# A Mamba-2 layer and a ternary FFN on one core: loops written out, opening and passage reordered

## The chip, the core and the metric

The kernel runs on one core of a Trainium2 chip. The core has a TensorE (PE, matrix products), a VectorE (DVE), a ScalarE (ACT), a GpSimd (POOL) and a SyncE (SP), which here only issues DMAs. Each engine has its own instruction stream, in order; they meet at semaphores alone. The time is device microseconds (us) of one execution. All data start and end in HBM.

## The reference

Input u is 2 sequences of 2048 tokens with 512 features. The result is the second of two blocks, each a layer, a residual and a layer norm:

```python
x = layernorm(u + attn(u));  out = layernorm(x + ffn(x))
# attn: state space layer (Mamba-2, SSD), 8 heads of 128, state 64
z, xBC, dt = split(u @ W_in.T);  dt = softplus(dt + dt_bias)
x, B, C = split(silu(causal_conv4(xBC) + conv_b))
dA = dt * -exp(A_log)                       # per head
y = ssd(x * dt, dA, B, C) + x * D           # h[t] = exp(dA[t]) h[t-1] + B[t] (dt x)[t];  y[t] = C[t] h[t]
yg = y * silu(z)
attn = (yg * rsqrt(mean(yg*yg) + 1e-5) * norm_w) @ W_out.T
# ffn: three weights W (2048 x 512) made ternary
q(W) = clip(round(W / s), -1, 1) * s,  s = mean(|W|) + 1e-8
ffn = (silu(x @ q(W_up).T) * (x @ q(W_gate).T)) @ q(W_down).T
```

## The kernel before

**Blocks.** The 4096 tokens are 8 blocks of 512, alternating between the two sequences; `par` is the sequence. Attention runs as steps n = 0..7, one per block, FFN as steps t = -1..7; t = -1 with its eight units q = 0..7 and what stands just ahead of it is the passage from one to the other. Products of f32 data are made from f16 high and low parts, three matmuls for one: so every weight piece needs a high part (ACT, `w_hi`) and a low part (`w_lo`, `w_lo_head`, in before all on DVE). A head tile, x or z of one head, is 12 matmuls into one of three PSUM banks that are used in turn (`RING`); eight other products share the bank `p_turn` in the order of `USES`.

**A step** has four slots p = 0..3 of two heads each. In a slot PE makes x and z of heads 2p and 2p+1 and, for the two heads of the slot before, transposes x (`turn_x`), makes the chunk states (`states`) and the outputs (`outputs`). x of a head passes ACT `conv_in`, DVE `conv` (three taps), ACT `conv_tanh`, DVE `silu`; then ACT `x_dt` scales the transposed x by dt. Of the next block, slots 1 to 3 also make B, C (`cb_tile`, `cb_conv`, `cb_silu`, whose outputs are `b_ch` and `c_ch`; `turn_b` and `cb` on PE read them) and dt (`dt_first`, `dt_second`, `dt_third`, then the cumulated sums). `cum_turned` copies these sums to `cum_t`, SP stores them (`store_cum`) and loads them back broadcast over partitions (`load_cum`, four DMAs per slot); ACT needs them for the decays (`growth`, `decays`). In slot 1 of step n the out projection of block n-1 is made, four chunks (`chunk_out`), each followed on DVE by `residual` (which adds `u_tok`, loaded by SP `load_utok`), its statistics, and `normalise`; `store_x1` writes the result.

**Weights of the FFN.** Their mean magnitude needs all 24 pieces of 512 KB of `w_ffn`: `load_abs(i)` on SP brings piece i into one of two buffers, and ACT (even i) or DVE (odd i) sums it (`magnitude(i)`, tile `abs_sum`). `load_abs(i)` waits until magnitude i-2 is done:

```python
if i >= 2:
    sp.wait_ge(abs_ok[i % 2], i // 2)
```

SP issues its DMAs in order, so whatever stands behind such a wait stands still too. SP's order in steps 0 and 1: slot (0,3) ends with `load_abs(8)` to `(11)`; then, opening step 1, `store_cum(1)` and `load_cum(1,0)`, in slot (1,0) `load_abs(12)`, `load_abs(13)`, `load_cum(1,1)`, and then `load_u(2)` and two `load_utok`. `load_abs(18)` and `(19)` stand ahead of `store_x1(0,0)` and `load_utok(0,2)`. From step 2 on the weights are made ternary (`quantise`, `factor_sums`) and stored.

**The FFN** works on one unit q of a block in seven products of sums and differences of quarter matrices (as Strassen's: `product`, names c11, c12, c21, c22, s1, u2, u3 for what is combined; ACT `chain_read` copies a product out of PSUM, DVE `summed` combines). `x_high`, `x_low`, `turn_x` on SP (DMA transposes) and `x_sum` prepare a block's input. `last_chunk` and `attention_rest` carry the last block's attention through t = -1.

**Loops.** The order of the work is written out by hand, per engine. Steps 0, 1, 6 and 7 are straight code; steps 2 to 5 are a register loop of two steps on every engine, and so are FFN steps 2 to 5:

```python
step(0, 0); step(1, 1)
with eng.Fori(0, QN // 2) as i:
    step(i * 2 + Q0, 0)
    step(i * 2 + (Q0 + 1), 1)
step(NB - 2, 0); step(NB - 1, 1)
```

In them a wait compares with a register's value, and `wait_apart` adds an increment of a semaphore behind it.

## Time and profile before

| | us |
|---|---|
| median of 3 runs | 1370.12 (1369.99 to 1370.62) |
| profiled execution, its own time | 1370.94 |
| its span | 1369.2 |
| PE busy | 1333.5 (97% of the span) |
| DVE / ACT / POOL busy | 1041.0 / 784.3 / 650.3 |
| granted TensorE clock, mean | 0.996 |

The busy time of an engine is the sum of its instructions; what lies between them is idle time, and the trace names for each idle stretch the instruction whose semaphore ended it. Only idle time of the engine that bounds the kernel costs time by itself. A granted clock of 1.00 is 2.4 GHz, 0.50 is 1.2 GHz. The opening is the span's first 175 us (steps 0 and 1), the register loops follow, the passage lies at about 680 to 800 us, and the FFN fills the rest.

### The profile page before, as it was taken

To read this page: it belongs to the slowest core of one execution; us is meant where nothing else is said; L and a number is where in the kernel's file an instruction comes from. 1 tells how busy PE (TensorE), PEld (TensorE's weight loads), DVE (VectorE), ACT (ScalarE), POOL (GpSimd) and SP (SyncE) were. 2 spreads that over 40 slices of the span, in tenths; PEclk is the share of its full clock that TensorE was granted. 3 is DMA by queue.
4 is the path that set the end of the run, shared out by engine and by line. 5 is a ranking of instruction groups with operands and counts; after the bars stand their busy time and mean duration, and the time that the engine had idled before them with its cause. 6 is when DMAs were issued, how large, how long until landed. Compare 5 with 4: busy or idle time off the path is not lost.

```text
span 1369.2 us, 26933 instructions
## 1 busy us (share of the span) xinstructions
PE 1333.5 (97%) x9318; PEld 866.4 (63%) x9318; DVE 1041.0 (76%) x1857; ACT 784.3 (57%) x1561; POOL 650.3 (47%) x634
## 2 busy tenths in 40 slices
PE   7899999999999999999999999999999999999998
PEld 4455565655555646556556677777777767777774
DVE  7887887887878868788684877777777767777775
ACT  6796673874757828658474555454544545454441
POOL 0575364673755837536255534353443424353331
PEclk9899999999999999999999999999999999999999
DMA  8537334353442633424546332223122322222002
GB/s 245 167 132 228 131 110 116 89 160 101 126 127 82 174 88 99 150 86 147 142 115 214 88 118 56 72 63 85 48 62 67 74 68 56 73 62 55 32 25 69
DMA packets 162796, 143.83 MB, mean 105 GB/s; under 512 B 101344, under 2 KB 123232, under 8 KB 161504
## 3 DMA queue, kind: packets, MB, share of 16 engines
q1 hardware_dynamic: 162656, 142.05, 36.1%
q8 instruction: 78, 1.28, 0.4%
q14 instruction: 62, 0.51, 0.1%
HBM read 99.93 MB, written 27.39 MB: 93 GB/s over the span
## 4 chain that ended last, share of the span: by engine, by line
PE 80%; DVE 7%; issue 4%; DMA 3%; ACT 2%; POOL 2%; SPq 1%; POOLq 0%; DVEq 0%; ACTq 0%
PE ring L936 20%; PE ring L1151 15%; PE ring L965 8%; PE p_turn L1131 7%; PE p_y L1131 7%; PE p_st L1131 6%; PE p_seg L1131 5%; PE p_y L1009 3%; PE p_y L1017 2%; PE p_st L999 2%; DMA quant<-in_w_ffn 2%; PE p_turn L989 1%; DVE acc L1804 1%; PE ring L1188 1%; DVE abs_sum L1782 1%
## 5 line engine op out<-in xcount | busy, mean ns | idle before, releaser
L936 PE MATMUL ring<-u_split,weights 128*128 128x512 f16 x1620 | 375.0, 382 | 2.2 <-DVE x_ch L1809 2.0
L936 PEld LDWEIGHTS ring<-u_split,weights 128*128 128x128 f16 x1620 | 154.9, 99 | 171.9 <-issue 6.6
L1713 POOL TENSOR_TENSOR xdt<-xdt 128x512 f32<-128x512 f32 x64 | 100.6, 1571 | 340.0 <-DVE xdt L2175 340.0
L965 PE MATMUL ring<-w_out,raw 128*128 128x512 f16 x672 | 147.3, 379 | 0.2 <-issue 0.2
L1804 DVE SCALAR_TENSOR_TENSOR acc<-ring,taps,acc 128x511 f32<-128x511 f32 (+2 forms) x192 | 143.7, 749 | 4.5
L965 PEld LDWEIGHTS ring<-w_out,raw 128*128 128x128 f16 x672 | 65.7, 98 | 79.5 <-issue 0.7
L1359 ACT ACTIVATE xdt<-p_turn,dts 128x128 f32<-128x128 f32 x256 | 72.7, 375 | 70.3 <-PE p_turn L989 70.3
L1620 POOL TENSOR_TENSOR raw<-yg,raw 128x512 f16<-128x512 f32 x64 | 78.8, 1231 | 65.9 <-ACT raw L1389 65.8
L1615 POOL TENSOR_TENSOR yg<-y_ch,z_ch 128x512 f32<-128x512 f32 x64 | 81.4, 1273 | 41.4 <-DVE y_ch L1929 41.4
L1368 ACT ACTIVATE p_seg<-cum_rows,cum 128x128 f32<-128x128 f32 x256 | 80.8, 389 | 8.7 <-DVE seg L1907 8.7
L1591 POOL TENSOR_TENSOR rstd<-var_e,exponent 128x1 f32<-128x1 f32 x32 | 20.2, 631 | 118.4 <-DVE var_e L1952 118.4
L1312 ACT ACTIVATE ring<-acc 128x512 f32<-128x512 f32 x64 | 38.7, 604 | 64.7 <-DVE acc L1804 63.6
L1628 POOL TENSOR_TENSOR sq_sum<-sq_sum,sq 128x512 f32<-128x512 f32 x56 | 71.3, 1273 | 0.0
L1009 PEld LDWEIGHTS p_y<-seg,xdt 128*128 128x128 f32 x512 | 62.4, 192 | 6.7 <-DVE seg L1907 2.3
L1520 ACT ACTIVATE cum_g<-c_dec,tanh_scale 128x512 f32<-128x512 f32 x32 | 23.1, 722 | 73.4 <-DVE b_dec L2167 73.4
L1009 PE MATMUL p_y<-seg,xdt 128*128 128x128 f32 x512 | 63.4, 276 | 1.7 <-DVE seg L1907 1.6
L1520 ACT ACTIVATE cum_g<-b_dec,tanh_scale 128x512 f32<-128x512 f32 x32 | 23.1, 722 | 70.1 <-DVE c_dec L2167 69.6
L1907 DVE TENSOR_TENSOR seg<-p_seg,cb_mask 128x512 f32<-128x512 f32 x64 | 43.9, 685 | 19.4 <-ACT p_seg L1372 19.3
L1520 ACT ACTIVATE grow<-xdt,tanh_scale 128x512 f32<-128x512 f32 x64 | 45.9, 718 | 19.5 <-DVE xdt L2167 19.0
L1838 DVE SCALAR_TENSOR_TENSOR z_ch<-thz,ring 128x512 f32<-128x512 f32 x64 | 43.8, 684 | 16.6 <-ACT thz L1328 14.3
L1809 DVE SCALAR_TENSOR_TENSOR x_ch<-ring,acc 128x512 f32<-128x512 f32 x64 | 44.0, 688 | 14.4 <-ACT ring L1312 14.0
L2167 DVE TENSOR_TENSOR xdt<-grow,p_turn 128x512 f32<-128x512 f32 x64 | 44.0, 687 | 13.3 <-ACT grow L1511 8.3
(395 smaller groups left out, 3246.7 us busy)
## 6 DMA issues: line engine op xcount, KB each, us to landing
cum_rows<-cum_dram SPq DMA_DIRECT2D x64, 256.0 KB, 4.1
quant<-in_w_ffn SPq DMA_DIRECT2D x24, 512.0 KB, 4.4
quant<-in_w_ffn SPq DMA_DIRECT2D x48, 256.0 KB, 4.1
cum_g<-cum_dram SPq DMA_DIRECT2D x64, 128.0 KB, 4.4
rows<-in_u_tok SPq DMA_DIRECT2D x32, 256.0 KB, 4.5
x_dram<-rows SPq DMA_DIRECT2D x32, 256.0 KB, 2.1
tern_ug<-quant SPq DMA_DIRECT2D x32, 256.0 KB, 3.3
u_raw<-in_u_t SPq DMA_DIRECT2D x7, 1024.0 KB, 8.7
```

The lines of the kernel that those rows point to most:

```text
L936: mm = pe.matmul(bank_k[:, :], w_in[:, ws, k, col:col + P], us[:, par, k * T:(k + 1) * T], start=(i == 0), stop=(i == 3 * KD - 1))
L965: mm = pe.matmul(ring[b][:, :], ys[:, h, c * P:(c + 1) * P], w_out[:, ws, h, :], start=(h == 0 and ys is y_hi and ws == 0), stop=(h == H - ...
L1009: pe.matmul(p_y[q][:, c * P:(c + 1) * P], xdt[:, q, c, :], seg[:, q, c, :], start=(c == 0), stop=False, skip_group_check=True)
L1131: mm = pe.matmul(bank_j[:, w * 256:(w + 1) * 256], factor(weight, w, k, q), xs[par][i][:, k, :], start=(first and w == 0 and k == 0 and xs ...
L1151: mm = pe.matmul(p_down[c % 2][:, :], hidden_tile(par, m, low)[:, c * P:(c + 1) * P], t_down(m), start=(e == 0 and m == 0 and not low), st ...
L1359: ins = act.activation(xdt[:, q, c, :], p_turn[:, c * P:(c + 1) * P], ACT.Copy, scale=dts[:, owner, c, h:h + 1])
L1368: ins = act.activation(p_seg[:, c * P:(c + 1) * P], cum_b[:, (2 * p - 2 + q) % 4, c, :], ACT.Relu, bias=cum[:, owner, h, c:c + 1], scale=-1.0)
L1520: act.activation(th[second], up, ACT.Tanh, scale=tanh_scale[:, 0:1]).then_inc(tanh_ok, 1)
L1615: pool.tensor_tensor(yg[:, q, :], y_ch[:, q, :], z_ch[:, k % 4, :], ALU.mult).then_inc(yg_ok, 1)
L1620: pool.tensor_tensor(y_lo[:, h, :], yg[:, q, :], y_hi[:, h, :], ALU.subtract).then_inc(ylo_ok, 1)
L1713: pool.tensor_tensor(tile_[:, 1, :, :], tile_[:, 0, :, :], tile_[:, 1, :, :], ALU.mult).then_inc(hid_ok, 1)
L1804: dve.scalar_tensor_tensor(acc[:, buf, k + 1:T], own[:, 0:T - 1 - k], taps[:, h, 2 - k:3 - k], acc[:, buf, k + 1:T], ALU.mult, ALU.add).th ...
```

## The change

**No loops.** `run_steps` and `ffn_steps` call `step` for each n and t in turn, on all five engines; every wait is on a constant, `wait_apart` and its increments are gone.

```diff
-            step(0, 0)
-            step(1, 1)
-            with eng.Fori(0, QN // 2) as i:
-                step(i * 2 + Q0, 0)
-                step(i * 2 + (Q0 + 1), 1)
-            step(NB - 2, 0)
-            step(NB - 1, 1)
+            for n in range(NB):
+                step(n, n % 2)
```

**Opening.** The low parts of heads 2, 3 and 7 are made by POOL in two instructions each, 2 and 3 first in its stream, 7 between the scaling and the low part of the first half of `w_out`. `cb_silu` makes b_ch first, and PE's `turn_b` waits for that alone, `cb` for all three. DVE's slot (0,2) is written out. The pieces below are of GpSimd, PE and DVE, in this order:

```diff
+            def w_lo_head(h):
+                own, k = raw_head(h), POOL_HEADS.index(h)
+                pool.wait_ge(w_hi_ok, head_piece(h) + 1)
+                pool.tensor_scalar(own, own, SW, None, ALU.mult).then_inc(w_mul_ok, 1)
+                pool.wait_ge(w_mul_ok, k + 1)
+                pool.tensor_tensor(w_in[:, 1, :, 2 * P * h:2 * P * (h + 1)], own, w_in[:, 0, :, 2 * P * h:2 * P * (h + 1)],
+                                   ALU.subtract).then_inc(w_half_ok, 1)
...
             def turn_b(n, use):
-                wait_apart(pe, bc_ok, n * 3 + 3, passed["pe"])
-                wait_apart(pe, turn_free, use, passed["pe"])
+                wait(pe, bc_ok, n * 3 + 1)
+                wait(pe, turn_free, use)
...
             cum_turned(0, turn_use(0, "cumt0"))
-            w_lo_head(2, w_half_ok)
-            cb_silu(0, 0, p_y[0])
+            cb_silu(0, 0, p_y[0], False)
             z_gate(0, 0)
-            w_lo_head(3, w_lo_ok)
+            conv(0, 0, 1)
             b_read(0, 0, turn_use(0, "b0"))
-            conv(0, 0, 1)
+            c_silu(0, 0, p_y[0])
...
+            magnitude(1)
             w_lo(4)
-            magnitude(1)
-            w_lo(5)
-            cb_conv(1, 1, ring[ring_bank("cb", 0)])
-            dt_second(1)
+            def second_slot():
+                n, par, p = 0, 0, 2
+                skip(n, p, 0)
+                skip(n, p, 1)
+                state_update(n, par, p - 1, C - 1)
+                cb_conv(1, 1, ring[ring_bank("cb", 0)])
+                dt_sum(1)
+                within(n, par, p, 0)
+                cb_silu(1, 1, ring[ring_bank("cb", 0)])
...
+                conv(n, par, 2 * p)
+                b_read(1, 1, turn_use(0, "b"))
+                dt_third(1, 1)
+                silu(n, 2 * p)
+                z_gate(n, 2 * p)
+                cum_read(1, 1, turn_use(0, "cum"))
+                w_lo_head(6)
+                conv(n, par, 2 * p + 1)
```

The slot of DVE at n = 0, p = 2 before, from its first `y_ch` (the skip term of the outputs) on; `carry` is the last chunk's state, `acc` the convolution:

```order
L1929 SCALAR_TENSOR_TENSOR y_ch<-x_ch,d_skip,p_y 128x512 [waits y_full]
L1929 SCALAR_TENSOR_TENSOR y_ch<-x_ch,d_skip,p_y 128x512
L1921 SCALAR_TENSOR_TENSOR carry<-st,grow,p_st 128x128 [waits st_ok]
L1907 TENSOR_TENSOR seg<-p_seg,cb_mask 128x512 [waits e_ok]
L1829 SCALAR_TENSOR_TENSOR c_ch<-ring,acc 64x512 [waits thc_ok]
L1829 SCALAR_TENSOR_TENSOR c_ch<-ring,acc 64x512
L1831 SCALAR_TENSOR_TENSOR b_ch<-ring,acc 64x512
L1782 TENSOR_REDUCE abs_sum<-quant 128x1 [waits abs_in1]
L1799 SCALAR_TENSOR_TENSOR acc<-ring,taps,corr 128x3 [waits acc_ok]
L1801 COPY halo<-ring 128x3
L1804 SCALAR_TENSOR_TENSOR acc<-ring,taps,acc 128x511 [waits tap_ok]
L1804 SCALAR_TENSOR_TENSOR acc<-ring,taps,acc 128x510 [waits tap_ok]
```

And after; the convolution with L1848 is that of B and C, which stood ahead of the slot before:

```order
L1966 SCALAR_TENSOR_TENSOR y_ch<-x_ch,d_skip,p_y 128x512 [waits y_full]
L1966 SCALAR_TENSOR_TENSOR y_ch<-x_ch,d_skip,p_y 128x512
L1958 SCALAR_TENSOR_TENSOR carry<-st,grow,p_st 128x128 [waits st_ok]
L1843 SCALAR_TENSOR_TENSOR acc<-ring,taps,corr 128x3 [waits accc_ok]
L1845 COPY halo<-ring 128x3
L1848 SCALAR_TENSOR_TENSOR acc<-ring,taps,acc 128x511 [waits tapc_ok]
L1848 SCALAR_TENSOR_TENSOR acc<-ring,taps,acc 128x510 [waits tapc_ok]
L1848 SCALAR_TENSOR_TENSOR acc<-ring,taps,acc 128x509 [waits tapc_ok]
L1893 TENSOR_SCALAR dt_w<-dt_e 128x32 [waits dt_a]
L1944 TENSOR_TENSOR seg<-p_seg,cb_mask 128x512 [waits e_ok]
L1855 SCALAR_TENSOR_TENSOR b_ch<-ring,acc 64x512 [waits thc_ok]
L1863 SCALAR_TENSOR_TENSOR c_ch<-ring,acc 64x512 x2
```

The skips and the carry have moved ahead of the convolution of B and C, and b_ch ahead of c_ch; the magnitude behind b_ch is gone from here.

The odd magnitudes stand one place later (`odd_rows`). Before, those of slot (0,2) were 3 and 5, of (0,3) 7 and 9, of (1,0) 11 and 13, of (1,1) 15, 17 and 19; now they are 3, then 5 and 7, then 9 and 11, then 13, 15, 17 and 19. Ahead of the second `cum_t` of DVE's stream, that of block 1, four rows of `abs_sum` stood, now three. In slot (1,1) magnitude 17 has a place of its own behind the dt steps. DVE there before, from `dt_w` on (`rows` with `mv,rstd` is `normalise`, with `ring,rms` is `residual`; `utok_in0` is the load of u_tok):

```order
L1859 TENSOR_SCALAR dt_w<-dt_e 128x32 [waits dt_a]
L1861 TENSOR_SCALAR dt_m<-dt_w 128x32 [waits dt_v]
L1863 RECIPROCAL dt_r<-dt_m 128x32 [waits dt_v]
L1956 TENSOR_SCALAR rows<-rows,mv,rstd 128x512 [waits rstd_ok]
L1944 SCALAR_TENSOR_TENSOR rows<-ring,rms,rows 128x512 [waits x1_out0,utok_in0,chunk_full]
L1947 BN_STATS stats<-rows 128x6 [waits chunk_ok]
L1949 BN_AGGR mv<-stats 128x2 [waits stat_ok]
L1952 TENSOR_SCALAR var_e<-mv 128x1 [waits mv_ok]
L1782 TENSOR_REDUCE abs_sum<-quant 128x1 [waits abs_in1]
```

And after:

```order
L1893 TENSOR_SCALAR dt_w<-dt_e 128x32 [waits dt_a]
L1898 TENSOR_SCALAR dt_m<-dt_w 128x32 [waits dt_v]
L1900 RECIPROCAL dt_r<-dt_m 128x32 [waits dt_v]
L1809 TENSOR_REDUCE abs_sum<-quant 128x1 [waits abs_in1]
L1993 TENSOR_SCALAR rows<-rows,mv,rstd 128x512 [waits rstd_ok]
L1981 SCALAR_TENSOR_TENSOR rows<-ring,rms,rows 128x512 [waits x1_out0,utok_in0,chunk_full]
L1984 BN_STATS stats<-rows 128x6 [waits chunk_ok]
L1986 BN_AGGR mv<-stats 128x2 [waits stat_ok]
L1989 TENSOR_SCALAR var_e<-mv 128x1 [waits mv_ok]
L1809 TENSOR_REDUCE abs_sum<-quant 128x1 [waits abs_in1]
```

A magnitude now stands ahead of `normalise(0,1)` and `residual(0,2)`, beside the one behind the statistics.

On SP in the same steps `load_wout(1)` has moved ahead of `load_abs(4)`, and `load_cum(1,1)` ahead of `load_abs(13)`; `store_cum(1)` stays behind `load_abs(11)`, and `store_x1(0,0)` with `load_utok(0,2)` behind `load_abs(19)`. In ACT's slot (0,2) `cb_tanh(1)` and `x_dt` of the second head stand ahead of `conv_in(4)`, `dt_ln(1)` ahead of the magnitude, and `conv_in(5)` ahead of the gating.

**Passage.** On SP (step 7, slot 2) the store and load of a chunk of block 6 stand between the transposes of block 0's input:

```diff
                             if is_at(n, NB - 1):
-                                for j in range(4):
+                                for j in range(2):
                                     turn_x(0, 0, j)
                             store_x1(n - 1, 0)
                             load_utok(n - 1, 2)
                             if is_at(n, NB - 1):
-                                turn_x(0, 0, 4)
+                                for j in range(2, 4):
+                                    turn_x(0, 0, j)
                             store_x1(n - 1, 1)
                             load_utok(n - 1, 3)
+                            if is_at(n, NB - 1):
+                                turn_x(0, 0, 4)
```

PE makes product 5 ahead of product 6, ACT reads u3 and s1 ahead of gating heads, and at t = -1 `residual` 0 and 3 stand ahead of the sum c12 on DVE, residual 3 at q = 7 instead of 6. POOL makes rms ahead of `hidden` there. The pieces are of PE, ACT, the table of `attention_rest`, POOL and DVE:

```diff
             product(0, 0, 0, 1, True)
+            pe.wait_ge(turn_free, turn_use(NB, "x01") + 1)
+            product(0, 0, 0, 5, True)
             pe.wait_ge(s1_ok, 1)
             product(0, 0, 0, 6, False)
-            pe.wait_ge(turn_free, turn_use(NB, "x01") + 1)
-            product(0, 0, 0, 5, True)
...
             gated(NB, 0, 1)
+            chain_read(0, 0, u3, prod[7], u3_ok, c21_ok)
             act.wait_ge(scales_ok, 3)
             gated(NB, 1, 0)
+            chain_read(0, 1, s1, prod[1], s1_ok, c11_ok)
             gated(NB, 1, 1)
...
-            return {2: 0, 3: 1, 4: 2, 6: 3}.get(q) if is_at(t, -1) else None
+            return {2: 0, 3: 1, 4: 2, 7: 3}.get(q) if is_at(t, -1) else None
...
                         if is_at(t, -1) and q == 2:
                             pool.wait_ge(ms_ok, 1)
                             pool.tensor_tensor(rms[:, :], ms[:, :], exponent[:, :], ALU.pow).then_inc(rms_ok, 1)
...
+                        hidden(m, k, True)
                         hidden(m, k, False)
...
+                    if attention_rest(t, q) in (0, 3):
+                        residual(NB - 1, attention_rest(t, q), p_down[attention_rest(t, q) % 2])
                     if before:
                         summed(m, k, "c12", u2, u2_ok, 5, ALU.add)
```

At t = -1 also the first half of `hidden` stands ahead of `x_low` on DVE, and `x_high` behind the first `hidden_tanh` on ACT. In step 7, slot 1, DVE makes `normalise` 0 and `residual` 1 ahead of `x_low` 2 and 3.

## Rows read from the trace of the kernel before

**Rows 1.** The page's summary: busy us, share of the span and instructions of each engine.
```profile
PE 1333.5 (97%) x9318; PEld 866.4 (63%) x9318; DVE 1041.0 (76%) x1857; ACT 784.3 (57%) x1561; POOL 650.3 (47%) x634
```

**Rows 2.** Waits of PE, costliest first: line, releaser, us in total, times, longest.
```profile
PE p_turn L974 <- DVE b_ch L1831: 4.6, 2, 4.0
PE p_st L999 <- DVE carry L1921: 4.3, 2, 2.3
```

**Rows 3.** PE in order of time, opening: start, us, line, operation, idle and releaser.
```profile
63.87 0.69 PE L974 MATMUL p_turn<-ident,b_ch 64*128 64x64 f32 x4 [3.97 <-DVE b_ch L1831]
...
73.36 0.81 PE L936 MATMUL ring<-u_split,weights 128*128 128x512 f16 x3
...
112.66 0.63 PE L989 MATMUL p_turn<-ident,x_ch 128*128 128x128 f32 x4 [0.18 <-ACT xdt L1359]
```

**Rows 4.** PE in order of time, its gaps in the rest of the run.
```profile
362.72 0.65 PE L989 MATMUL p_turn<-ident,x_ch 128*128 128x128 f32 x4 [0.98 <-issue]
...
689.29 0.99 PE L999 MATMUL p_st<-xdt,b_dec 128*64 128x128 f32 x14 [2.33 <-DVE carry L1921]
...
724.29 0.94 PE L1131 MATMUL ring<-b_tok,weights 128*128 128x256 f16 x7 [0.69 <-ACT cum_g L1511]
...
735.03 1.05 PE L1131 MATMUL p_turn<-c_ch,weights 128*128 128x256 f16 x8 [1.37 <-DVE xdt L2167]
...
754.33 2.76 PE L1188 MATMUL ring<-w_out,raw 128*128 128x512 f16 x12 [1.54 <-DVE rows L1944]
...
792.79 1.05 PE L1131 MATMUL p_turn<-c_ch,cum_rows 128*128 128x256 f16 x8 [1.45 <-DVE xdt L2167]
...
1105.36 0.83 PE L1131 MATMUL p_st<-acc,weights 128*128 128x256 f16 x6 [1.63 <-issue]
```

**Rows 5.** Two stretches: us, busy time of each engine, granted clock, DMA share, GB/s.
```profile
33.00:36.00 3.00, 3.00 (x9) 1.04 (x8) 2.93 (x7) 2.99 (x2) 0.00 (x0) 0.50 1.03 322
...
60.00:67.00 7.00, 3.13 (x10) 1.39 (x11) 5.11 (x9) 3.18 (x7) 2.71 (x4) 0.51 0.71 193
```

**Rows 6.** DVE in order of time, opening, step 1 and the passage.
```profile
25.70 0.69 DVE L1831 SCALAR_TENSOR_TENSOR b_ch<-p_y,acc 64x512 f32<-64x512 f32 x1
...
47.43 2.29 DVE L1770 SCALAR_TENSOR_TENSOR weights<-raw,weights 128x2048 f16<-128x2048 f32 x1
...
50.77 3.24 DVE L1770 SCALAR_TENSOR_TENSOR weights<-raw,weights 128x2048 f16<-128x2048 f32 x1
...
105.09 1.21 DVE L1782 TENSOR_REDUCE abs_sum<-quant 128x1 f32<-128x1024 f32 x1
...
146.09 0.75 DVE L1944 SCALAR_TENSOR_TENSOR rows<-ring,rms,rows 128x512 f32<-128x512 f32 x1
...
154.28 1.40 DVE L1929 SCALAR_TENSOR_TENSOR y_ch<-x_ch,d_skip,p_y 128x512 f32<-128x512 f32 x2
...
680.35 0.75 DVE L1944 SCALAR_TENSOR_TENSOR rows<-ring,rms,rows 128x512 f32<-128x512 f32 x1 [3.03 <-DMA rows<-in_u_tok]
```

**Rows 7.** POOL in order of time: low parts of the first half of w_out.
```profile
48.38 7.76 POOL L1672 TENSOR_TENSOR w_out<-rows,w_out 128x512 f16<-128x512 f32 x4 [3.79 <-ACT w_out L1289]
```

**Rows 8.** DMA issues of the queue engine SP in order of time, steps 0 and 1.
```profile
95.39 0.43 SPq L606 DMA_DIRECT2D cum_dram<-cum_t  x1
99.47 0.34 SPq L616 DMA_DIRECT2D cum_rows<-cum_dram  x1
...
104.85 0.33 SPq L598 DMA_DIRECT2D quant<-in_w_ffn  x1
...
140.05 0.43 SPq L622 DMA_DIRECT2D rows<-in_u_tok  x1
```

**Rows 9.** ACT in order of time, step 1 and the passage.
```profile
110.87 0.62 ACT L1351 ACTIVATE grow<-cum_g 128x512 f32<-128x512 f32 x1
...
733.61 0.58 ACT L1511 ACTIVATE grow<-ring 128x512 f32<-128x512 f32 x1
```

**Rows 10.** The page's DMA issues: tiles, engine, count, KB each, us to landing.
```profile
rows<-in_u_tok SPq DMA_DIRECT2D x32, 256.0 KB, 4.5
```

More of the change, by code:

```diff
@@ L1458, in step @@
                         decays(n, par, p, 0)
-                    if not end:
+                    if is_at(n, 0) and p == 2:
+                        cb_tanh(1, ring[ring_bank("cb", 0)])
+                        x_dt(n, par, p, 1)
                         conv_in(n, 2 * p)
-                    if state_slot(n, p):
+                        decays(n, par, p, 1)
+                        dt_ln(1)
+                    elif not end:
+                        conv_in(n, 2 * p)
+                    if state_slot(n, p) and not (is_at(n, 0) and p == 2):
                         x_dt(n, par, p, 1)
                         decays(n, par, p, 1)
-                    if is_at(n, 0) and p == 2:
-                        cb_tanh(1, ring[ring_bank("cb", 0)])
                     if abs_rows(n, p, 0) is not None:
@@ L1474, in step @@
                         split_u(n + 1, 1 - par)
-                    if p == 2 and more(n):
+                    if p == 2 and more(n) and not is_at(n, 0):
                         dt_ln(n + 1)
@@ L1478, in step @@
                         magnitude(abs_rows(n, p, 1))
-                    if not end:
+                    if not end and not (is_at(n, 0) and p == 2):
                         conv_in(n, 2 * p + 1)
@@ L1551, in ffn_step @@
                         m, its, k = before
+                    if before and not (is_at(t, -1) and q == 1):
                         wait(act, act_ok, 2 * (m * NQ + k) - 1)
@@ L1700, in step @@
                         rms_root(n - 1, turn_use(n, "ssq"))
-                    if quantised(n) and not isinstance(n, int):
+                    if quantised(n) and n < NB - 2:
                         factor_sums(n, p)
@@ L1827, in cb_silu, with c_silu @@
                     dve.wait_ge(cdec_ok, n * NP - NP)
+                dve.scalar_tensor_tensor(b_ch[:, :], b[N:P, :], 1.0, acc[N:P, 2, :], ALU.add,
+                                         ALU.mult).then_inc(bc_ok, 1)
+                if both:
+                    c_silu(n, par, b)
+            def c_silu(n, par, b):
                 for half in range(2):
@@ L2046, in _ @@
             dt_first(1, turn_use(0, "dt"))
+            magnitude(1)
             w_lo(4)
[L2048 to L2051 removed]
+            def second_slot():
[7 more added lines that the diff above has]
+                cb_silu(1, 1, ring[ring_bank("cb", 0)])
+                dt_inverse(1)
+                for c in range(C - 1):
+                    state_update(n, par, p, c)
+                within(n, par, p, 1)
+                conv(n, par, 2 * p)
[6 more added lines that the diff above has]
+                conv(n, par, 2 * p + 1)
+                silu(n, 2 * p + 1)
+                magnitude(3)
+            second_slot()
             def step(n, par):
                 first, end = is_at(n, 0), is_at(n, NB)
[L2055 removed]
+                for p in range(3 if first else 0, 4):
                     if gate_slot(n, p):
@@ L2065, in step @@
                         within(n, par, p, 0)
-                    if first and p == 2:
-                        cb_silu(1, 1, ring[ring_bank("cb", 0)])
-                    if abs_rows(n, p, 0) is not None:
-                        magnitude(abs_rows(n, p, 0) + 1)
                     if not end:
@@ L2143, in step @@
                         dt_second(n + 1)
+                    if odd_rows(n, p, 2) is not None:
+                        magnitude(odd_rows(n, p, 2))
                     if p == 1 and not first:
@@ L2258, in ffn_step @@
                         summed(n, q, "c11", s1, s1_ok, 2, ALU.add)
+                    if is_at(t, -1) and before:
+                        hidden(m, k, True)
                     for j in splits_at(t, q):
@@ L2268, in ffn_step @@
                     if before:
-                        hidden(m, k, True)
+                        if not is_at(t, -1):
+                            hidden(m, k, True)
                         hidden(m, k, False)
```

195 lines of the change are left out of this document (103 added, 92 removed).

## The prediction

> **What bounds the kernel now.** I read the engine summary first. TensorE (PE) is busy 97% of the span [rows 1], so only time in which PE stands still, or runs slower, can be won. The waits by engine come next: PE waits 4.6 us for b_ch and 4.3 us for a carry [rows 2], always two waits together. Then PE in order of time, which puts them: 3.97 us of the b_ch wait lies at 63.87, so z of head 5 starts only at 73.36 [rows 3]; 2.33 us of the carry wait stands ahead of 689.29 [rows 4]. Outside the first 175 us, the passage from attention to FFN (680 to 800 us) and the last 9 us PE has no gap over 0.3 us but two: 0.98 us at 362.72 and 1.63 us at 1105.36, put down to "issue" [rows 4]; there the register loops of PE and the other engines turn. Last the granted clock by stretch: it is 0.50, 1.2 GHz, at 33 to 36 us and 0.51 on average at 60 to 67 us, each after or around a PE idle [rows 5].
>
> **Part 1: no loops.** PE's two boundary gaps go: -0.98 and -1.63 us. The extra semaphore increments and register arithmetic sit on queues that PE does not wait for (the steps inside the loops show no "issue" gap over 0.3 us), so I take nothing for them. The whole part is -2.6 us. The lower bound is those gaps, since what the other engines lose there is behind PE's work; the upper one is zero, if the gap is PE fetching a far stretch of code that straight code fetches too. I take -2.6, because steps 0, 1, 6 and 7, already straight code, have no such gap in PE's rows. The Trainium skill says the same from the other side (Runtime: NRT & Kernel Launch, Instruction fetch mechanics): a taken branch breaks the sequential prefetch, so straight code has no such stall; by it the term is the whole -2.6 as well.
>
> **Part 2: the opening.** b_ch comes first on DVE, the low parts of heads 2, 3 and 7 leave DVE, and its slot (0,2) is written out. Walked forward with the durations of before:
> - b_ch stood behind a low part (1.2) and two c_ch (1.4) and started at 25.70 [rows 6]; PE's turn_b moves up by 0.7. With two low parts of a head less on DVE (1.2 each), z of head 2 moves up by 2.8 and x of head 4, which needs w_lo(4), by 3.4, to 47.7.
> - w_lo(5), 3.24 us at 50.77, is gone and the skips stand ahead of the B/C convolution, so states(0,2) moves up by 5.5 to 53.3, and turn_b(1) from 63.87 to 54.4; head 5's z starts at 61.3 instead of 73.36, 12.1 us earlier. Here DVE and ACT are late in turn: conv 5 has been put behind dt_third, cum_read and the low part of head 6, so the next turn_x moves up by 8.8 only, to 69.5. PE stands about 2.5 us before it and some of the next tiles run at half clock. The gain that arrives at step 1 is 8.3 to 9 us.
>
> One row bears on this sum: w_lo(5) took 3.24 us where w_lo(4), the same shape, took 2.29, and it ran while POOL did the four low parts of w_out in 7.76 us [rows 6, 7]. The Trainium skill (SBUF — State Buffer, SBUF: two separate sides) says that a DVE instruction with two SBUF inputs and a GpSimd one reading SBUF exclude each other for a whole instruction. By it, and the trace agrees with its 3.24 against 2.29, head 7's POOL part beside w_lo(4) would take up to 0.95 us of the gain at x of head 4; what I take is none, and the next part shows why it would not reach the end.
>
> **Queue block A.** The odd magnitudes come one place later on DVE: ahead of the second cum_t there are now three, not four. SP issues DMAs in order, and a load_abs(i) waits for magnitude i-2. load_abs(11), ahead of store_cum(1), now waits for magnitude 9, which sits where magnitude 11 stood, 105.09 [rows 6], less the 8.3 gained: it ends at 98.0. store_cum goes at 98.5 instead of 95.39; it lands 4.1 later by before (95.39 to the first cum_rows at 99.47 [rows 8]), 2.2 in the first block, so I take 3.1: four loads end at 103.6. Only then load_abs(12), at 104.85 before [rows 8]; it lands 4.4 to 5.2 later, 108.0 to 108.8. ACT does magnitude 12 ahead of growth(1,1) and x_dt, 110.87 before [rows 9]. So growth starts at 109.6 to 110.4, and PE's turn_x, 112.66 before [rows 3], at 111.4 to 112.1: of 8.3 us some 0.5 to 1.3 are left. PE idles about 8 us here, and the two stretches of 1.2 GHz (3.0 and 3.5 us long, costing half of that each [rows 5]) say that the clock falls after such a gap: +1.4. Balance after A: -0.5 + 1.4, about +1.
>
> **Queue block B.** magnitude 17 now stands after the dt steps of step 1, ahead of normalise(0,1) and residual(0,2), at 145.6 to 146.8. load_abs(19) waits for it, and behind it on SP stand store_x1(0,0) and load_utok(0,2), issued at 140.05 before [rows 8], now at 147.65. With 3.9 to 4.5 us to land (4.5 is the page's median [rows 10]) it is there at 151.5 to 152.2, and residual(0,2), 146.09 before [rows 6], waits for it. Behind it on DVE: its statistics (1.0), magnitude 19 (1.2), normalise (0.55), residual 3 with statistics (1.8), 0.66 for rstd and normalise 3. skip(1,2) comes at 158.5, not 154.28 [rows 6]: +4.2. PE's states had 1.3 us in hand, cum_proj behind it less: +2.9 there, +3.7 to 4.1 in all. B costs +4 (2.5 to 5). From step 2 on DVE catches up and PE keeps the loss.
>
> Opening together: +5; from -1, where either block is half as bad, to +8 with another stretch at 1.2 GHz.
>
> **Part 3: the passage.** PE's gaps, and what is late next:
> - 2.33 at 689.29 [rows 4]: the carry stood behind residual 2, which waited 3.03 us for its u_tok at 680.35 [rows 6], a load behind four transposes on SP. Now only two lie ahead. All 2.33 go.
> - 0.69 at 724.29: product 5 now fills it. 1.37 at 735.03: xdt waited for ACT's u3 at 733.61, behind the gating of two heads [rows 4, 9]; moved ahead of them it is done by 730. 1.54 at 754.33: the last chunk waited for a residual that waited for POOL's rms, which now goes ahead of a hidden of 1.65 us. 1.45 at 792.79: DVE's xdt stood behind residual 3.
> - Two small ones between the first and the second, 0.6 together, move with the first.
>
> Sum -8.0. But at q=7 of t=-1 residual 3 is now ahead of c12 and takes 0.75 plus 1.0 us of statistics there: +1.1. Residual 0 ahead of c12 at q=2 does the same unless rms is early. I take -6 (-3 to -7.5).
>
> **Sum.** The profiled execution took 1370.94 us. -2.6 + 5 - 6 = -3.6 gives 1367.3; it lay 0.8 over the median of the runs shown (1370.12), so by the median 1366.5. I say 1366.4.
>
> **Rivals.**
> - The queue blocks don't bite, because the DMAs land sooner than I took or magnitudes 9 and 17 are early enough: then 8 us stay from the opening, and with -2.6 and -6 it is 1353 to 1358. For it: the walk to 63.87 rests on durations alone. Against it: the SP queue is in order, and both waits are plain in the order. 0.13.
> - Nothing that can be measured: the passage only gives 3 of its 8, since PE waits for c12 or for the down product's residual instead, and the opening costs 4: 1367.5 to 1372.5. For it: each passage gap is under 2.4 us and the next producer is often 0.5 to 1 us behind. 0.28.
> - Slower: SP's in-order queue. If store_cum takes its 4.1 us (+1), B costs 5 (+1), and PE runs two further stretches of 3.0 to 3.5 us at 1.2 GHz behind these idles (+1.7 each), the opening is +10.4. Against -2.6 and the least that I allow the passage, -3, that is +4.8: 1375 (1373 to 1376). It decides from an opening of +8.3 on. For it: both waits are plain in the order, and neither is hidden behind another engine's work. Against it: PE's idle and the low clock overlap in part. 0.12.
> - The change doesn't do what it says in part 1: straight code stalls as the loop did; then 1369, within the second rival.
>
> **From these to the numbers.** Forecast (1360 to 1367.4) 0.47. A run can tell from no change about 0.2%, 2.7 us. Faster: 0.47 + 0.13 = 0.60; same 0.28; slower 0.12. Range 1357 to 1373: below it most of the first rival, above it most of the last. The forecast's own range is 1362 to 1369.
>
> **What would show it.** Loops: no "issue" gap of PE near 362 or 1105. Opening: turn_b(1) at about 54, head 5's z at about 61, a PE gap of some 8 us ending near 112 with a DMA of w_ffn ahead of it; store_cum(1) issued at 98, not at 87; load_utok(0,2) near 147.6 and DVE's residual waiting for it. If PE has no gap near 104 to 112, the first rival holds. Passage: states at the place of 689.29 without a gap, xdt no longer behind u3, a small new PE gap at q=7. It is wrong if block 1's loads land before ACT needs them, or if the passage keeps gaps of more than 4 us in sum.

## The result and the profile after

The changed kernel takes 1372.93 us, the median of 11 executions (1370.55 to 1373.87), against 1370.12 (1369.70 to 1371.08): the ratio is 1.0017, with a 95% interval of 1.0009 to 1.0025. It is slower by 2.8 us, where 3.7 us less were forecast; a second set of 11 executions gave 1373.35 against 1370.32 (ratio 1.0018, 1.0009 to 1.0027). Its profiled execution took 1370.55 us with a span of 1368.4, less than all others of both sets: the trace shows the change at its best, and what the others have beside it is a question of its own, below.

Where PE stands at the same piece of work in the two traces:

| work | before | changed | difference |
|---|---|---|---|
| z of head 5 | 73.36 | 62.35 | -11.0 |
| turn_x(1,1,1) | 112.66 | 113.51 | +0.9 |
| states(1,2) | 157.22 | 162.49 | +5.3 |
| product of the magnitudes' sums | 171.38 | 177.75 | +6.4 |
| first tile behind the loop's boundary | 363.21 | 368.54 | +5.3 |
| states(7,2) | 689.29 | 692.37 | +3.1 |
| chunk 1 in the passage | 754.33 | 752.48 | -1.9 |
| product at q = 7 of t = -1 | 792.79 | 791.60 | -1.2 |
| first product behind the FFN loop's boundary | 1105.36 | 1104.21 | -1.2 |

The opening won 11 us by 73 us and was 0.9 behind at 113. PE in order of time in the changed kernel, at the places of [rows 3] and behind them (in brackets the idle time ahead and what ended it):

```profile
55.36 0.46 PE L973 MATMUL p_turn<-ident,b_ch 64*128 64x64 f32 x4
...
62.35 2.76 PE L935 MATMUL ring<-u_split,weights 128*128 128x512 f16 x12
...
113.51 1.08 PE L989 MATMUL p_turn<-ident,x_ch 128*128 128x128 f32 x4 [8.72 <-ACT xdt L1359]
114.38 3.84 PE L935 MATMUL ring<-u_split,weights 128*128 128x512 f16 x12
...
162.49 1.09 PE L999 MATMUL p_st<-xdt,b_dec 128*64 128x128 f32 x16 [3.52 <-DVE carry L1958]
```

turn_b(1) has no wait left. But a gap of 8.72 us has come ahead of turn_x(1,1,1), the 12 matmuls behind it take 3.84 us where they take 2.75 elsewhere, and states(1,2) waits 3.52 us for a carry. What each waits for shows first on SP, answering to [rows 8] (the second number is the issue's own time):

```profile
99.02 0.98 SPq L601 DMA_DIRECT2D cum_dram<-cum_t  x1
102.75 0.33 SPq L611 DMA_DIRECT2D cum_rows<-cum_dram  x1
...
105.49 0.58 SPq L593 DMA_DIRECT2D quant<-in_w_ffn  x1
...
149.70 0.42 SPq L617 DMA_DIRECT2D rows<-in_u_tok  x1
```

and on ACT, answering to [rows 9]:

```profile
110.18 1.06 ACT L1293 ACTIVATE quant<-quant 128x1024 f32<-128x1024 f32 x1 [8.45 <-DMA quant<-in_w_ffn]
...
111.71 0.62 ACT L1351 ACTIVATE grow<-cum_g 128x512 f32<-128x512 f32 x1
```

and on DVE, answering to [rows 6]; the first row is magnitude 9:

```profile
97.40 1.21 DVE L1809 TENSOR_REDUCE abs_sum<-quant 128x1 f32<-128x1024 f32 x1
...
154.31 0.75 DVE L1981 SCALAR_TENSOR_TENSOR rows<-ring,rms,rows 128x512 f32<-128x512 f32 x1 [5.34 <-DMA rows<-in_u_tok]
...
160.69 1.40 DVE L1966 SCALAR_TENSOR_TENSOR y_ch<-x_ch,d_skip,p_y 128x512 f32<-128x512 f32 x2
```

store_cum(1) goes at 99.02, behind load_abs(11), which magnitude 9 releases at 98.5; its loads go from 102.75, and load_abs(12) at 105.49. ACT is through with its work at 101.7 and stands 8.45 us for that piece, with growth(1,1) and x_dt behind it, and PE behind x_dt. In the second block load_utok(0,2) goes at 149.70 instead of 140.05 and residual(0,2) waits 5.34 us for it.

The passage's gaps, answering to [rows 4]:

```profile
692.37 1.09 PE L999 MATMUL p_st<-xdt,b_dec 128*64 128x128 f32 x16
...
752.48 2.75 PE L1188 MATMUL ring<-w_out,raw 128*128 128x512 f16 x12
...
791.60 1.05 PE L1131 MATMUL p_turn<-c_ch,cum_rows 128*128 128x256 f16 x8 [1.50 <-DVE xdt L2222]
...
795.30 1.05 PE L1131 MATMUL p_turn<-u_raw,u_split 128*128 128x256 f16 x8 [0.90 <-DVE c_dec L2222]
...
797.20 1.05 PE L1131 MATMUL p_seg<-u_raw,u_split 128*128 128x256 f16 x8 [0.85 <-ACT cum_g L1518]
```

Those at 689.29, 724.29, 735.03 and 754.33 are gone, that at 792.79 has stayed with 1.50 us, and two new ones of 0.90 and 0.85 us stand behind it. A third new one, 0.53 us on DVE's xdt, stands at 765.57.

### The profile page after: what moved, and what is told of

Same layout as the page of the kernel before. It is cut to its first block, busy times and chain, and to the rows that moved or that the text cites. A ratio compares the mean times of both kernels' runs of the same rounds, so it can differ in the third digit from the quotient of the medians.

```text
span 1368.4 us, 24907 instructions
## 1 busy us (share of the span) xinstructions
PE 1331.5 (97%) x9318; PEld 867.0 (63%) x9318; DVE 1046.1 (76%) x1855; ACT 785.2 (57%) x1561; POOL 666.7 (49%) x640
## 4 chain that ended last, share of the span: by engine, by line
PE 82%; DVE 8%; issue 4%; ACT 2%; POOL 2%; DMA 1%; SPq 0%; POOLq 0%; DVEq 0%; ACTq 0%
PE ring L935 20%; PE ring L1151 15%; PE ring L964 9%; PE p_turn L1131 7%; PE p_y L1131 7%; PE p_st L1131 6%; PE p_seg L1131 6%; PE p_y L1009 3%; PE p_y L1017 2%; PE p_st L999 2%; PE p_turn L989 2%; DVE acc L1831 1%; PE ring L1188 1%; DMA raw<-in_w_in 1%; POOL sq_sum L1643 1%
## 5 line engine op out<-in xcount | busy, mean ns | idle before, releaser
L1307 ACT ACTIVATE acc<-ring,tap_bias,taps 128x512 f32<-128x512 f32 x64 | 49.5, 774 | 6.7 <-PE ring L935 6.4
```

## The experiments

Each kernel was timed beside the kernel before on the same chip; the median of the latter was 1370.32 for e1 to e4, 1370.31 for e5 to e8, 1369.86 for e9 to e12 and 1370.39 for e13 and e14. So a difference of two medians from different groups carries up to some 0.5 us of its surroundings; where that matters, the difference from the kernel before is given instead. "A" is the block at 113 us, "B" that at 162.

### The change once more

No edit; a second trace.

> The changed kernel once more, unaltered, for a second trace: its profiled execution took 1370.55 us, but the median of its eleven runs is 1372.93 and the mean granted clock of the others is 0.990 to 0.995 against 0.997. Theory (clock after an idle): PE's idle of 8.7 us ahead of 113.5 us and that of 3.5 us ahead of 162.5 come in every execution, and how long PE then runs at 1.2 GHz differs between executions; so a trace of a run near 1373 has the same gaps on all engines and one or two more stretches of 3 to 7 us at a granted clock of 0.50, worth 2 to 3 us, behind these gaps. Rival (DMA): the slower executions have longer landings of w_ffn and u_tok, so the gaps themselves are 1 to 2 us longer at the same clock. Rival (code): the slower executions have 'issue' gaps of PE in the steps that were loops. Time 1372 to 1373.5.

1373.35 us (1371.12 to 1374.55, 11 runs). The profiled execution is a long one, span 1371.9. PE in it, and then the granted clock of both traces by stretch (us, busy times of the five engines, granted clock, DMA share, GB/s):

```profile
115.22 1.08 PE L989 MATMUL p_turn<-ident,x_ch 128*128 128x128 f32 x4 [9.66 <-ACT xdt L1359]
...
165.31 1.97 PE L999 MATMUL p_st<-xdt,b_dec 128*64 128x128 f32 x16 [3.97 <-DVE carry L1958]
```

```profile
60.00:80.00 20.00, 16.94 (x103) 9.21 (x102) 17.40 (x36) 16.88 (x39) 14.59 (x14) 0.91 0.45 148
...
106.00:121.00 15.00, 5.78 (x24) 2.89 (x26) 4.45 (x9) 8.69 (x24) 4.65 (x5) 0.66 0.94 296
...
160.00:175.00 15.00, 11.03 (x73) 7.00 (x70) 13.93 (x32) 9.36 (x19) 7.80 (x9) 0.77 0.57 179
```

```profile
60.00:80.00 20.00, 16.80 (x116) 10.14 (x116) 17.41 (x35) 17.50 (x41) 14.71 (x14) 1.00 0.41 140
...
106.00:121.00 15.00, 7.49 (x41) 3.96 (x42) 5.77 (x11) 10.76 (x28) 4.47 (x5) 0.77 0.87 286
...
160.00:175.00 15.00, 11.44 (x88) 7.80 (x89) 14.03 (x31) 11.37 (x21) 8.62 (x9) 1.00 0.67 211
```

The same gaps, 0.4 to 0.9 us longer; but the clock is 0.91, 0.66 and 0.77 (the first three rows) where the short execution has 1.00, 0.77 and 1.00. states(1,2), 1.09 us there, takes 1.97 here. Both theories have a share: the gaps differ a little, and this execution ran at 1.2 GHz behind the gaps at 71 and 162 us too. Of the 22 executions of the change two have a mean clock of 0.997, and they are the two fastest, 1370.55 and 1371.12; the rest lie at 0.990 to 0.995. No new gap put down to "issue" is there: the third theory falls.

### The loops, and the passage, by themselves

e2 writes out the two loops and changes nothing else; with the loops go the register comparisons and the extra increments in their waits. e3 adds all the edits of the passage to that. Of e2's edit, the attention loop:

```diff
-            with eng.Fori(0, QN // 2) as i:
-                step(i * 2 + Q0, 0)
-                step(i * 2 + (Q0 + 1), 1)
...
+            for n in range(NB):
+                step(n, n % 2)
```

> The kernel before with the register loops written out on all five engines and nothing else. Theory: the two boundary gaps of PE (0.98 and 1.63 us) go: 1367.0 to 1367.8, that is -2.3 to -3.0. Rival (straight code costs its own fetches): within 0.5 us of 1370.1, with new issue gaps of PE somewhere in steps 2 to 5. Rival (the loops hid a phase that now meets a slower clock): slower than 1371.

> As e2 with the reordered passage as well, the opening left as it was before. Theory from the two profiles: the passage alone gives 4.7 us on PE (PE was 5.3 us late ahead of it and 0.6 behind it), so 1362 to 1363.5; the opening of the change is then shown to cost 9 to 11 us by the medians. Rival (the passage gives what it gives only because the opening came late to it): 1365 to 1367.

e2: 1367.88 (1366.96 to 1368.68), ratio 0.9980 (0.9971 to 0.9989), -2.4 us, 0.1 above the range of its theory. The boundary in its trace, at the place of 362.72:

```profile
361.52 0.60 PE L978 MATMUL p_turn<-ident,x_ch 128*128 128x128 f32 x4
```

No gap, as forecast; the one at 1105.36 is gone too. e3: 1362.95 (1362.60 to 1363.50), ratio 0.9942 (0.9928 to 0.9955). The passage gives 4.9 us more, and the opening of the change, 1373.35 against 1362.95, costs 10.4. (The three terms add up to the whole change by the way they are taken, one after the other, so their sum checks nothing.)

### The two moves on the queue

e4 makes both, e5 that for A, e6 that for B. The diff shows the lines at their new places; the same lines are taken out at the old ones.

```diff
                         load_abs(10)
+                        store_cum(n + 1, 1 - par, turn_use(n, "cumt"))
+                        load_cum(n + 1, 1 - par, 0)
                         load_abs(11)
...
                         load_abs(18)
+                        store_x1(0, 0)
+                        load_utok(0, 2)
                         load_abs(19)
```

> The changed kernel with two moves on the queue engine alone: store_cum(1) and load_cum(1,0) ahead of load_abs(11), and store_x1(0,0) with load_utok(0,2) ahead of load_abs(19). Theory (the two queue blocks): PE's gap of 8.7 us at 113.5 shrinks to 1 to 3 us, since ACT's magnitude 12 gets its piece at about 104 instead of 110; residual 2 no longer waits 5.3 us at 154.3. PE at step 2 is then 6 to 8 us earlier than in the change before, and no stretch of 1.2 GHz stands behind 113: 1360 to 1364. Rival (the gap is DMA bandwidth, not the queue's order): the landing of w_ffn pieces and of the cum rows gets longer by as much, and it stays within 2 us of 1372.9.

> The changed kernel with the first of the two moves alone: store_cum(1) and load_cum(1,0) ahead of load_abs(11). Theory: PE's gap at 113.5 falls from 8.7 to about 3 us and the stretch at 1.2 GHz behind it gets shorter; residual(0,2) still waits some 5 us for its u_tok, since PE comes to block 2 earlier and DVE's magnitude 17 moves with it: 1366.5 to 1368.5. Rival (the second block takes back what the first gives, because load_abs(19) waits for a fixed DMA chain): within 1.5 us of 1373.

> The changed kernel with the second move alone: store_x1(0,0) and load_utok(0,2) ahead of load_abs(19). Theory: the gap at 113.5 stays at 8.7 to 9.7 us, residual(0,2) no longer waits 5.3 us, states(1,2) comes without its 3.5 to 4.0 us gap, and the stretch at 1.2 GHz that one of two traces shows behind that gap is gone: 1368.5 to 1370.5. Rival (B costs nothing by itself, DVE is as late without it): within 1 us of 1373.

e4 1364.12 (1362.82 to 1365.12), e5 1366.77 (1364.74 to 1368.38), e6 1368.92 (1367.24 to 1371.78). Against 1373.35 that is -9.2, -6.6 and -4.4. e5 and e6 lie inside what the theory gave, e4 0.1 above its upper edge; the rivals, all within 1 to 2 us of 1373, fall. With the magnitudes where the change has them, the order of the queue decides whether there is a block. The two moves do not add: 6.6 and 4.4 by themselves, 9.2 together, so the move for B is worth 4.4 with block A in place and 2.6 without it (why was not tested). In e5 and e6 the other block is still there, as the rows of PE show, of e5 first:

```profile
108.94 1.09 PE L991 MATMUL p_turn<-ident,x_ch 128*128 128x128 f32 x4 [3.97 <-ACT xdt L1361]
...
158.75 1.97 PE L1001 MATMUL p_st<-xdt,b_dec 128*64 128x128 f32 x16 [3.22 <-DVE carry L1960]
```

```profile
114.40 1.08 PE L992 MATMUL p_turn<-ident,x_ch 128*128 128x128 f32 x4 [9.32 <-ACT xdt L1362]
```

In e5 A has shrunk to 3.97 and B, 3.22, is nearly whole; in e6 A is whole and states(1,2) has no wait. What is left of A in e5 is ACT's magnitude 12, which stands 3.70 us for its piece of w_ffn in the trace. e8 moves that magnitude too:

```diff
-                     (1, 0): (None, 10, 12), (1, 1): (None, 14, 16, 18)
+                     (1, 0): (None, 10), (1, 1): (12, 14, 16, 18)
```

> As e4 with one more edit: ACT's magnitude 12 moves from the end of slot (1,0) to behind the decays of slot (1,1), so that growth(1,1) and x_dt do not stand behind its piece of w_ffn (in e4's trace it waited 2.9 us for it, and PE 3.15 us for x_dt, with 3 us at 1.2 GHz behind). Theory: that gap goes, 1360 to 1362 against e4's 1364.1. Rival (the pieces of w_ffn are a chain of their own: each later magnitude is a later load, and a DVE or ACT wait comes back further on): 1363 to 1365.

Four executions took 1358.13 to 1360.47, median 1359.8, 0.2 below the theory's range; a fifth took 4920, which nothing in its record explains, and is left out of the median. The gap ahead of turn_x(1,1,1) is gone in its trace.

### The magnitudes' places

e7 takes the change and puts the odd magnitudes where they were, the queue's order as in the change; e10 takes e3, opening and queue as before, and puts them one place later. Of e7:

```diff
-            rows_ = {(0, 3): (5, 7), (1, 0): (9, 11), (1, 1): (13, 15, 17, 19), (1, 2): (21, 23)}
+            rows_ = {(0, 3): (7, 9), (1, 0): (11, 13), (1, 1): (15, 17, None, 19), (1, 2): (21, 23)}
...
+                magnitude(3)
                 conv(n, par, 2 * p)
...
-                magnitude(3)
+                magnitude(5)
```

> The changed kernel with the odd magnitudes on DVE where they stood before (3 and 5 in slot (0,2), 7 and 9 in (0,3), 11 and 13 in (1,0), 15, 17 and 19 in (1,1)), the order of the queue engine as in the change. Theory (the later magnitudes are what blocks the queue): load_abs(11) is released by magnitude 9 near 86, store_cum goes at 87 to 88, both blocks are gone without touching the queue's order: 1361 to 1365; magnitude 3 ahead of conv(4) costs 1.2 us of DVE in a slot where PE waits for ACT anyway. Rival (the pieces land too late for such early magnitudes, so DVE waits for DMA in slot (0,2)): 1366 to 1370.

> e3 (no loops, reordered passage, opening as before) with one edit: the odd magnitudes on DVE one place later, exactly as in the change. Theory (this move alone makes both queue blocks): magnitude 9 ends near 106, store_cum goes behind it at 107 instead of 95.4, the loads of the cumulated sums come near 111 and ACT's growth(1,1) and PE's turn_x(1,1,1) at about 120 instead of 112.7; residual(0,2) waits for its u_tok too: 1372 to 1378, that is 9 to 15 over e3's 1363. Rival (the blocks need the earlier opening of the change to show): 1363 to 1366.

e7: 1360.42 (1360.30 to 1361.72), a little below what was expected; 12.9 us come back by this one edit; store_cum goes at 88.72 in its trace. e10: 1386.48 (1385.47 to 1386.84, four executions), +23.5 on e3, beyond the 9 to 15 expected. Its rows, of SP, then of POOL, then of PE:

```profile
75.31 0.43 SPq L586 DMA_DIRECT2D rows<-in_w_out  x1
...
112.14 1.12 SPq L601 DMA_DIRECT2D cum_dram<-cum_t  x1
```

```profile
81.45 4.03 POOL L1671 TENSOR_TENSOR rows<-rows,norm_s 128x512 f32<-128x512 f32 x4 [8.76 <-DMA rows<-in_w_out]
```

```profile
89.78 2.07 PE L1007 MATMUL p_y<-seg,xdt 128*128 128x128 f32 x8 [4.38 <-DVE seg L1915]
...
128.37 1.08 PE L987 MATMUL p_turn<-ident,x_ch 128*128 128x128 f32 x4 [10.22 <-ACT xdt L1357]
...
177.96 1.98 PE L997 MATMUL p_st<-xdt,b_dec 128*64 128x128 f32 x16 [3.48 <-DVE carry L1929]
```

The direction holds and the two blocks are the ones named, but magnitude 9 ends at 111.7, not at 106, since a third block stands ahead of them, 4.38 us at 89.78, with low clock behind it. Its rows show the queue once more: e10 has the queue of before, where load_wout(1) stands behind load_abs(5) and so behind magnitude 3, which is now later. It goes at 75.31, in e3 at 64.58; POOL waits 8.76 us for it with the scaling of w_out, ACT and DVE stand behind POOL's yg (3.73 and 4.97 us), and PE behind DVE. The change has moved this load ahead of load_abs(4), where it goes at 57.98. No run moves it by itself, so this third block is read from the rows and has no price of its own. The edit on the magnitudes costs 12.9 with the opening and queue of the change and 23.5 with those of before. So the reordered opening without this edit is worth 1362.95 - 1360.42 = 2.5 us, not the 8 to 9 that stand at 100 us: z of head 5 stands at 63.39 in e7, 9.1 us earlier than in e3, and the product of the magnitudes' sums at 167.60, 3.2 us earlier (170.76).

### The clock behind the gap

e9 is the change with 36 matmuls more in gap A, e13 is e6 with the same.

```diff
+                    if is_at(n, 1) and p == 1:
+                        pe.wait_ge(y_ok, n * H)
+                        for i in range(36):
+                            pe.matmul(p_y[0][:, :], w_in[:, 0, 0, 0:P], u_hi[:, par, 0:T], start=True, stop=True)
```

> The changed kernel with 36 further matmuls on PE (128x512, f16, about 7.8 us) in the gap ahead of turn_x(1,1,1), into the bank that the outputs of that slot overwrite later; their results are not used. They start once the skips of the slot are done (105.0 in the change's trace) and would end at about 113. Theory (the clock falls after the idle, and how long it stays low differs between executions): the granted clock stays 1.00 over 106 to 121, PE's next 12 matmuls take 2.75 us and not 3.84, and the median falls by 1.5 to 3 to 1370 to 1371.5. Rival (the low clock is not tied to this idle): the clock is 0.5 in the same stretch and the time is 1373 or more.

> e6 (only store_x1(0,0) and load_utok(0,2) moved ahead of load_abs(19)) with the 36 further matmuls of e9 in PE's remaining gap ahead of turn_x(1,1,1). e6 measured 1368.92 (1367.24 to 1371.78). Theory (the gap costs its own 8.7 us and then 1 to 2.5 us of low clock, different in each execution): with the gap filled the granted clock is 1.00 from 106 us to 175 us and the median is 1366.5 to 1367.5. Rival (the clock falls anywhere, this gap or not): 1368.5 to 1369.5.

e9: 1371.37 (1370.01 to 1375.54), 2.0 below the change by the medians as they stand, 1.5 when each is taken from the kernel before beside it. e13: 1367.66 (1367.01 to 1369.06), 1.3 below e6 by either way and 0.2 above the theory's 1367.5, and within 2.1 us where e6 spread over 4.5 (2.8 without its slowest one). PE in e9, then the clock in e9 and in e6:

```profile
106.59 7.94 PE L1090 MATMUL p_y<-u_split,weights 128*128 128x512 f16 x36 [0.91 <-DVE y_ch L1970]
115.26 0.63 PE L989 MATMUL p_turn<-ident,x_ch 128*128 128x128 f32 x4 [0.73 <-ACT xdt L1363]
115.72 2.75 PE L935 MATMUL ring<-u_split,weights 128*128 128x512 f16 x12
```

```profile
106.00:121.00 15.00, 13.49 (x74) 6.49 (x75) 4.82 (x10) 9.00 (x25) 4.87 (x5) 1.00 0.96 305
...
160.00:175.00 15.00, 12.24 (x85) 8.30 (x86) 13.53 (x30) 11.12 (x21) 8.88 (x9) 0.89 0.65 211
```

```profile
106.00:121.00 15.00, 6.60 (x33) 3.37 (x34) 4.46 (x9) 9.43 (x26) 4.17 (x5) 0.66 0.94 298
```

More work on PE in a gap makes the kernel faster, since the tile behind it takes 2.75 us and not 3.84 to 4.57. e9 still has B, and the clock there is 0.89; e13 has neither, and its clock is 1.00 from 106 to 175 us (its mean clock is 0.998 to 0.999 in all 11 executions, e6's 0.993 to 0.996).

### What is left, and the best version

e11 is e3 with residual 3 back at q = 6. e12 is the change with magnitudes 3 to 9 as before, 11 alone in (1,0), 13 to 19 in (1,1), and the move for B. e14 is e12 with the edits of e8 and e11.

```diff
-            return {2: 0, 3: 1, 4: 2, 7: 3}.get(q) if is_at(t, -1) else None
+            return {2: 0, 3: 1, 4: 2, 6: 3}.get(q) if is_at(t, -1) else None
...
+            rows_ = {(0, 3): (7, 9), (1, 0): (11,), (1, 1): (13, 15, 17, 19), (1, 2): (21, 23)}
```

> e3 with residual 3, its norm_root and normalise at q = 6 behind the sums, as before, the rest of the passage as in the change. It asks where the passage's missing 1.3 to 1.8 us went. Theory: the two new gaps of PE at q = 7 (0.90 on c_dec and 0.85 on ACT's p_seg read) are from residual 3 ahead of c12 and go: 1361 to 1361.8. Rival (they come from the end of the passage, the gap of 1.45 comes back beside them): 1363 to 1364.

> The change with magnitudes 3 and 5 in slot (0,2), 7 and 9 in (0,3) as before, but only 11 in (1,0) and 13, 15, 17, 19 in (1,1), and with store_x1(0,0) and load_utok(0,2) ahead of load_abs(19). In e7's trace DVE waited 4.7 us for piece 13 at the end of slot (1,0), with PE 1.9 and 0.9 us behind; here that wait goes. Theory: 1357 to 1359. Rival (the pieces are a chain, the wait comes back at magnitude 17 or 19): 1360 to 1362.

> e12 with ACT's magnitude 12 behind the decays of slot (1,1) (as in e8) and residual 3 at q = 6 (as in e11): all that the runs so far pointed to. Theory: e12 has no PE gap over 0.4 us between 76 and 160 us, so magnitude 12 gives nothing more, and residual 3 gives 0.3 to 1.2: 1359 to 1360. Rival (magnitude 12 behind the decays makes ACT late in slot (1,1)): 1360 to 1362.

e11: 1362.60 (1361.41 to 1362.96), above the theory's 1361.8 and 0.35 below e3, inside the spread of both (against the kernel before beside it, 7.3 below where e3 is 7.4 below). In its trace the two new gaps are gone, and the one on xdt has grown:

```profile
785.37 1.05 PE L1123 MATMUL p_turn<-c_ch,cum_rows 128*128 128x256 f16 x8 [2.06 <-DVE xdt L2167]
```

Against e3's 1.50, 0.90 and 0.85 us that is 1.2 us less in the trace; the medians don't confirm so much. e12: 1360.06 (1358.80 to 1361.09), above the 1357 to 1359 of the theory and no better than e7. The number is the rival's, but its wait is not there: PE has no gap over 0.4 us between 76 and 160 us. e12 reaches the tiles at 85 us some 1.8 us later than e7, and its trace has a stretch of low clock at 20 to 23 us that e7's has not; which of its edits makes it late was not tested. e14: 1358.76 (1357.31 to 1358.91), ratio 0.9910 (0.9896 to 0.9923): faster than both kernels, 11.6 us below the one before and 14.6 below the change, and 0.2 below what was expected. It is 1.7 below e7, which needs the one edit alone; four kernels (e7, e8, e12, e14) lie within that.

## Why the prediction was wrong

**The total.** 1366.4 was forecast, 1372.93 measured. By medians the three terms are -2.4 (forecast -2.6), -4.9 (forecast -6) and +10.4 (forecast +5). Loops: right. Passage: right in sign and place, 1.1 too much. The step that failed is the sum of the opening: "+5" from block A with its clock term (about +1) and block B (+4). Its mechanisms came; its sizes were too small. The traced executions show +6.4 at the product of the magnitudes' sums: PE reaches turn_x(1,1,1) 0.9 us late where -0.5 was forecast, the low clock behind costs 1.5 where 1.4 was forecast, and B brings the rest. Most of what is missing from there to +10.4 lies between the traced executions and the medians: the change's trace is 2.4 us faster than its median, that of before 0.8 us slower. So the term that was most mis-sized is, as far as the second trace of the change shows it, the low clock behind the idles, put at one stretch (+1.4) from one trace, with the arrival of block A (1.4) next. How much of those 3 us is low clock alone stays open in part: filling one gap gives 1.3 to 2.0 of them back.

**The walk to 73 us** held to 1.2 us: turn_b(1) was put at 54.4 and stood at 55.4, z of head 5 at 61.3 and stood at 62.35, the next turn_x at 69.5 and stood at 70.7 with an idle of 2.59 ahead. (The reading that PE has no gap over 0.3 us outside the places named passed over one of 0.35 us at 577.05; the forecast does not hang on it.) The exclusion that the Trainium skill states (SBUF — State Buffer, SBUF: two separate sides) was there, with the loser reversed. DVE's w_lo(4), and POOL's two instructions for head 7 in the changed kernel:

```profile
46.14 2.28 DVE L1798 SCALAR_TENSOR_TENSOR weights<-raw,weights 128x2048 f16<-128x2048 f32 x1
```

```profile
43.66 2.77 POOL L1676 TENSOR_SCALAR raw<-raw 128x1024 f32<-128x1024 f32 x1
46.52 3.90 POOL L1678 TENSOR_TENSOR weights<-raw,weights 128x1024 f16<-128x1024 f32 x1
```

w_lo(4) started first and took its 2.28 us; the subtraction beside it took 3.90 where those of heads 2 and 3 took 2.14 and 2.13. The 0.95 us that I left out of the sum were rightly left out at this place. At another, 35.36, DVE's split of u took 3.29 us beside POOL's c_dec where it took 2.28 before with POOL idle; the forecast had nothing for that.

**Queue block A** was named with its chain, and each link came: magnitude 9 at 98.0 (98.5), store_cum at 98.5 (99.02), load_abs(12) at 103.6 (105.49), growth(1,1) at 109.6 to 110.4 (111.71), PE at 111.4 to 112.1 (113.51). The miss of 1.4 us and more is a sum of small ones: the store landed after 3.7 us where I took 3.1, the four loads took 2.7 to issue where I took 2.0, and the piece landed in 4.7. I had chosen the middle between the store of the first block, 2.2, and that of the place itself, 4.1; the row of the same place was the nearer one.

**The clock behind A** was taken as +1.4, from the two stretches of before. One such stretch behind one gap is what the fast trace shows (3.84 for 2.75, and the turn 1.08 for 0.63, 1.5 in all). The second trace, 3.5 us longer, has three: 1.3 to 2.0 us of median came back when gap A was filled, and states(1,2) at half clock is 0.9 us more, with the tiles behind it. That the untraced executions differ in the same way is argued from their mean clocks (0.990 to 0.995), not seen. The prediction took one trace for the kernel. Of before this was nearly true, 1369.7 to 1371.1 in the runs of the result, though single ones beside the experiments took 1373.13 and 1373.79 at a mean clock of 0.993 and 0.992.

**Queue block B** was put at +4 (2.5 to 5). In the fast trace PE was 1.7 us behind just ahead of its gap and 5.3 at the states, which makes 3.6, and 6.4 at the product behind, which makes 4.7; by e6 it costs 4.4. The chain came as told: residual(0,2) waiting for its u_tok, 5.34 us, skip(1,2) at 160.69 where 158.5 was forecast.

**The rivals.** The one that came is "slower", given 0.12: its opening of +10.4 is the measured one, and it was to lead to 1375 with a passage of -3; with the measured -4.9 it is 1373.1. That it agrees to the decimal is luck: the store took 3.7 and not 4.1, B 4.4 and not 5. What it had right is that all the terms err to one side. The prediction gave it a small chance because the idle and the low clock "overlap in part". In the traces they come one behind the other: the clock is low while PE works again, so its cost is added to the gap's. The first rival, that the blocks do not bite, is refuted by e4 to e7; that straight code stalls as the loop did, by e2.

**Where the passage's other 1.1 us are.** -8.0 was the sum of the gaps, of which 1.45 at 792.79 did not go (1.50 now, with residual 3 no longer ahead of DVE's xdt; what holds it there instead I did not test). The +1.1 for residual 3 ahead of c12 at q = 7 came as two gaps of 0.90 and 0.85, and the 0.53 at 765.57 was not forecast. With all, -8.0 + 1.5 + 1.75 + 0.5 is -4.2, and 4.9 by the medians; the 0.7 between them no gap in the rows accounts for.

## What to carry to other kernels

Before moving a piece of filler work on one engine, list what its semaphore releases on an in-order queue and what stands behind that release: here reductions of 1.2 us each, moved one place later to make room on DVE, held back a store and a load that ACT, DVE and PE waited for, and cost 13 us. Either cure works: the old places of the reductions (e7), or the store and loads ahead of the waits and one more reduction moved (e8). A gain early in a pipeline is not a gain at its end: of 9.1 us at z of head 5, 3.2 were left at 168 us and 2.5 in the time, even with both blocks gone. And a forecast for PE after an idle stretch needs a second price, that of the low clock behind it, with a range of its own, since one profiled execution may be the fortunate one.
